# The sixth tile's down products in two matmuls instead of three, with the low half stacked beside the high half

## The chip, the cores and the metric

One core of a Trainium2 chip runs the whole program. The metric is the device time of one execution in microseconds. Before the change it is 1329.63 us, the median of 3 runs (1329.51 to 1329.85). Engines are named as in the profile: PE does matmuls (PEld its weight loads), DVE and POOL do elementwise work, ACT does activations, SP issues the DMAs.

## What is computed

A macaron block over 2048 tokens of 256 channels, in float32:

```
x = x + 0.5 * ffn(layernorm(x))
x = x + mamba2(layernorm(x))
x = x + 0.5 * ffn(layernorm(x))
ffn(x):  h = silu(x @ gate.T) * (x @ up.T);  return h @ down.T      # gate, up: 688 x 256, down: 256 x 688
```

The FFN's weights are drawn from a table of 16 values (`lut[idx]`). The change touches both FFNs and the passage from the first FFN into the Mamba part.

## The kernel before, in words

**Split products.** Every large product is made in three passes. Each operand is rounded to a high half (type fp32r) and its rest, the low half, and `split_matmul` (L35 to L40) adds hi times hi (L38), hi times lo (L39) and lo times hi (L40) in PSUM.

**The FFN.** Its 688 inner columns are six tiles of 128; the sixth (m = 5, `MT - 1`) has 48 columns and zeros behind them. Tokens come in four tiles of 512 (T). One pair of T and m is a tick, k = 6 T + m, so each FFN has 24 ticks. In tick k PE makes gate and up products of tile k (`ffn_in`, 12 matmuls of 512 columns; in a sixth tile the up columns lie in the gate tile's rows 64 to 111, so there are 6), then transposes or side work (`before_down`), and then the down products of tile k - 2 (`ffn_down(k - 2)`, 12 matmuls of 256 columns: 3 passes for each of 4 token groups of 128). ACT makes silu of the gate product and later `ffn_hidden_hi`, the high half of the product h (L668); DVE multiplies (L1129, in a sixth tile L1125 on 64 rows); POOL makes `ffn_hidden_lo` (L961). The second FFN is the class `TickFfn`, with the same split of work (L97, L103, L109, L117, L121).

**What PE waits for in the first FFN.** The up products of tick k go to the bank that silu of tick k - 1 read, so they wait for `silu_done` k (at m > 0). The transposes of the next token tile's normalised rows xn (L205; at k = 1, 3, 5) wait for DVE, which writes xn (L196) after its product of ticks 0, 2 and 4. Down products wait for the low half.

**Work woven into the first FFN.** ACT splits one Mamba weight tile, `xw_raw` to `xw_hi` (L680), after `ffn_hidden_hi` in each of ticks 0 to 3, and waits there for that tile's DMA. POOL makes `xw_lo` (L967) behind it. The buffer `xw_raw` has two places, so the loads of tiles 2 and 3 (L535) can start only when POOL is done with tiles 0 and 1. From tick 9 on Mamba's B, C and dt are made beside the FFN's ticks: projection on PE, a causal convolution on DVE (`taps_bc`, L1167 and L1171), silu on ACT.

**The queue of SP** is strictly in order. After the first loads it stores the decoded FFN weights for the second FFN (`spill`, L555: gate, up, then down_hi and down_lo), and behind these stand the loads of `xw_raw` 2 and 3.

**After tick 23** comes the passage into the Mamba loop (`fill(-8)`): turn_B and make_CB for token tile 2, the first x and gate projections, and the last layer norm: ACT's silu of CT, the rows of cum and e, B_tok, a square root (L178), then DVE's xn (L196) and PE's transposes.

## Time and profile before

| | |
|---|---|
| median of 3 runs | 1329.63 us |
| the profiled execution | 1329.74 us, its span 1328.0 us |
| PE busy | 1281.5 us, 96% |
| DVE busy | 1185.5 us, 89% |
| ACT busy | 999.6 us, 75% |
| POOL busy | 891.7 us, 67% |

Times in rows count from the span's start. The first FFN lies at 76 to 196 us, the Mamba loop between about 204 and 1219, the second FFN at 1219 to the end. A matmul's busy time is longer than the distance to the next one's start, since matmuls overlap; what one costs is read from start to start.

### The profile page before, as it was taken

How to read it: one execution, taken by the hardware profiler on the slowest of the kernel's cores; microseconds unless marked ns; L12 is line 12 of the kernel's file. 1: busy time of each engine (PE TensorE's matmuls, PEld its weight loads, DVE VectorE, ACT ScalarE, POOL GpSimd, SP SyncE). 2: the span in 40 equal slices, each digit the busy share in tenths (PEclk: the TensorE clock that was granted, in tenths of full speed). 3: DMA queues.
4: the chain of work that ended last, by engine and by line, in shares of the span. 5: the costliest groups of instructions: out<-in, count | busy, mean ns of one | idle time of the engine just before them, and what ended most of it. 6: DMA issues, size and time to landing. Idle time of an engine off the chain costs nothing.

```text
span 1328.0 us, 26759 instructions
## 1 busy us (share of the span) xinstructions
PE 1281.5 (96%) x8784; PEld 1080.8 (81%) x8784; DVE 1185.5 (89%) x2652; ACT 999.6 (75%) x2044; POOL 891.7 (67%) x920
## 2 busy tenths in 40 slices
PE   7999998899999999999999999999999999997998
PEld 7988886678888888887888888888878888876887
DVE  7965577899999999999999999999999999997542
ACT  1135567888888888888888888888888888883442
POOL 1033220279798988888797989888887979785332
PEclk9999999999999999999999999999999999998999
DMA  7031002365654643545655556445445654435000
GB/s 166 2 151 33 17 28 62 73 136 131 112 123 117 133 116 110 119 108 110 114 132 116 120 124 122 122 109 119 108 108 113 132 124 114 104 104 214 16 17 33
DMA packets 98105, 136.49 MB, mean 103 GB/s; under 512 B 23760, under 2 KB 45872, under 8 KB 97840
## 3 DMA queue, kind: packets, MB, share of 16 engines
q1 hardware_dynamic: 97968, 134.78, 42.7%
q8 instruction: 72, 1.18, 0.4%
q14 instruction: 65, 0.53, 0.1%
HBM read 124.78 MB, written 9.96 MB: 101 GB/s over the span
## 4 chain that ended last, share of the span: by engine, by line
PE 71%; DVE 17%; issue 7%; ACT 3%; POOL 1%; DMA 0%; DVEq 0%; POOLq 0%; SPq 0%; ACTq 0%
PE psum L38 15%; PE psum L40 13%; PE psum L39 13%; PE psum L1749 9%; PE psum L1726 7%; PE psum L1738 6%; PE psum L1527 4%; PE psum L1715 4%; DVE inner L1346 2%; DVE xs L1294 2%; DVE xdt L1304 2%; DVE xend L1312 2%; DVE mixed L1376 1%; DVE M L1322 1%; DVE carry L1346 1%
## 5 line engine op out<-in xcount | busy, mean ns | idle before, releaser
L848 ACT ACTIVATE M<-cum_row,cum_table 128x128 f32<-128x128 f32 x1024 | 312.1, 389 | 0.0
L1294 DVE SCALAR_TENSOR_TENSOR xs<-psum,conv_w_sb,xs 128x509 f32<-128x509 f32 (+2 forms) x384 | 282.2, 735 | 0.4
L1056 POOL TENSOR_TENSOR hid<-hid,sg 128x512 f32<-128x512 f32 x128 | 165.6, 1294 | 86.3 <-DVE hid L1363 86.3
L1007 POOL CAST hid_hi<-hid 128x512 fp32r<-128x512 f32 x128 | 194.0, 1516 | 8.2
L1042 POOL TENSOR_TENSOR squares<-squares,sq 128x512 f32<-128x512 f32 x124 | 161.1, 1299 | 53.3 <-ACT sq L825 53.3
L1322 DVE TENSOR_TENSOR M<-M,CB 128x1024 f32<-128x1024 f32 x128 | 187.7, 1467 | 0.0
L862 ACT ACTIVATE xs<-psum,conv_b_sb,conv_w_sb 128x512 f32<-128x512 f32 x128 | 99.1, 774 | 105.0 <-PE psum L40 66.9
L1010 POOL TENSOR_TENSOR hid_lo<-hid,hid_hi 128x512 fp32r<-128x512 f32 x128 | 166.2, 1299 | 10.2
L1749 PEld LDWEIGHTS psum<-M,xdt 128*64 128x64 f32 x2048 | 109.9, 137 | 45.9 <-issue 45.9
L1726 PE MATMUL psum<-xend,B_tok 128*128 128x128 f32 x960 | 132.0, 279 | 10.6 <-DVE carry L1346 9.8
L1749 PE MATMUL psum<-M,xdt 128*64 128x128 f32 x2048 | 140.8, 280 | 0.8 <-DVE psum L1354 0.7
L856 ACT ACTIVATE M<-M 128x1024 f32<-128x1024 f32 x128 | 134.5, 1051 | 0.5
L1726 PEld LDWEIGHTS psum<-xend,B_tok 128*128 128x128 f32 x960 | 117.6, 192 | 16.4 <-DVE xend L1312 8.3
L961 POOL TENSOR_TENSOR ffn_hidden_lo<-ffn_hidden,ffn_hidden_hi 128x512 fp32r<-128x512 f32 x24 | 31.2, 1301 | 132.6 <-ACT ffn_hidden_hi L668 132.6
L1346 DVE SCALAR_TENSOR_TENSOR inner<-inner,decay_table,psum 128x64 f32<-128x64 f32 x512 | 116.7, 267 | 0.0
L38 PE MATMUL psum<-xT_hi,gw_hi 128*128 128x512 f32 x256 | 111.7, 436 | 4.9 <-issue 4.9
L38 PE MATMUL psum<-xT_hi,xw_hi 128*128 128x512 f32 x256 | 113.4, 443 | 0.0
L1738 PE MATMUL psum<-CT,inner 128*128 128x128 f32 x768 | 107.2, 276 | 1.3 <-DVE inner L1346 0.8
L38 PE MATMUL psum<-hid_hi,wo_hi 128*128 128x512 f32 x256 | 100.9, 394 | 4.6 <-issue 3.9
L1738 PEld LDWEIGHTS psum<-CT,inner 128*128 128x128 f32 x768 | 97.6, 191 | 5.6 <-DVE inner L1346 2.1
L40 PE MATMUL psum<-xT_hi,xw_lo 128*128 128x512 f32 x256 | 101.1, 395 | 0.0
L40 PE MATMUL psum<-xT_hi,gw_lo 128*128 128x512 f32 x256 | 100.7, 393 | 0.0
(201 smaller groups left out, 3308.1 us busy)
## 6 DMA issues: line engine op xcount, KB each, us to landing
cum_row<-cum_scratch SPq DMA_DIRECT2D x256, 256.0 KB, 4.7
e_row<-e_scratch SPq DMA_DIRECT2D x256, 128.0 KB, 4.1
xw_raw<-L_attn_in_proj_w_dram SPq DMA_DIRECT2D x32, 128.0 KB, 4.8
wo_raw<-L_attn_out_proj_w_dram SPq DMA_DIRECT2D x32, 128.0 KB, 4.6
gw_raw<-L_attn_in_proj_w_dram SPq DMA_DIRECT2D x16, 256.0 KB, 5.0
x_res<-_attn_hidden_states_dram SPq DMA_DIRECT2D x4, 512.0 KB, 7.8
x_scratch<-x_res SPq DMA_DIRECT2D x4, 512.0 KB, 2.6
x_res<-x_scratch SPq DMA_DIRECT2D x1, 2048.0 KB, 10.5
```

Source lines behind the costliest of these rows:

```text
L38: nc.tensor.matmul(out, l_hi, r_hi, start=start, stop=False, skip_group_check=skip)
L39: nc.tensor.matmul(out, l_hi, r_lo, start=False, stop=False, skip_group_check=skip)
L40: return nc.tensor.matmul(out, l_lo, r_hi, start=False, stop=stop, skip_group_check=skip)
L848: last = nc.scalar.activation(M[:, v % 3, h, c * CH:(c + 1) * CH], cum_row[:, v % 2, h, c * CH:(c + 1) * CH], ACT.Relu, bias=scalar_of(CUM ...
L1007: nc.gpsimd.tensor_copy(hid_hi[:, v % 2, :], hid[:, v % 2, :]).then_inc(hid_hi_done, 1)
L1010: nc.gpsimd.tensor_tensor(hid_lo[:], hid[:, v % 2, :], hid_hi[:, v % 2, :].bitcast(F32), ALU.subtract).then_inc(hid_lo_done, 1)
L1056: nc.gpsimd.tensor_tensor(hid[:, v % 2, :], hid[:, v % 2, :], sg[:, v % 8, :], ALU.mult).then_inc(hid_done, 1)
L1294: nc.vector.scalar_tensor_tensor(xs[:, v % 7, shift:], psum[:, X_BANK + v % 2, 0:TT - shift], tap_of(v, step), xs[:, v % 7, shift:], ALU.m ...
L1322: nc.vector.tensor_tensor(M[:, v % 3], M[:, v % 3], cb, ALU.mult).then_inc(M_done, 1)
L1726: last = nc.tensor.matmul(psum[:, ST_BANK, c * P:(c + 1) * P], B_tok[:, t * CPT + c, :], xend[:, c].rearrange("p h q -> p (h q)"), start=T ...
L1738: last = nc.tensor.matmul(psum[:, Y_BANK, c * CH:(c + 1) * CH], before.rearrange("p h q -> p (h q)"), CT[:, tok:tok + CH], start=(c == fir ...
L1749: last = nc.tensor.matmul(psum[h * HP:(h + 1) * HP, Y_BANK, c * CH:(c + 1) * CH], xdt[:, v % 2, c, h, :], M[:, v % 3, h, c * CH:(c + 1) * CH],
```

## The change

For a sixth tile only 48 rows of h are real, so the 64 rows below them are free. ACT now writes the high half to rows 0 to 63 alone, and DVE writes the low half to rows 64 to 127 of the same tile (`ffn_tail_lo`); POOL has nothing to do there. The rows 64 to 127 of `down_hi`'s sixth tile get a copy of its rows 0 to 63, once, on DVE at k = 2; those of `down_lo` stay zero. One matmul with `down_hi` then adds hi times hi and lo times hi, a second with `down_lo` hi times lo: 8 matmuls for a sixth tile where there were 12. The store of down_hi waits for the copy (`doubled`). In `fill(-8)` the first x projection is moved ahead of turn_B and make_CB.

```
+def stacked_matmul(nc, out, both, w_hi, w_lo):
+    nc.tensor.matmul(out, both, w_hi, start=False, stop=False, skip_group_check=True)
+    return nc.tensor.matmul(out, both, w_lo, start=False, stop=True, skip_group_check=True)
...
     def pool_lo(self, pool, k):
+        if k % MT == MT - 1:
+            return
...
@@ def spill(i), on SP
                 if i == 0:
                     sp.wait_ge(tail_done, 2)
+                if i == 2:
+                    sp.wait_ge(doubled, 1)
...
@@ def ffn_hi(k), on ACT
-                nc.scalar.activation(f_hi[:, k % 3, :], f_h[:, k % 2, :], ACT.Copy).then_inc(f_hi_done, 1)
+                rows = slice(0, HP if k % MT == MT - 1 else P)
+                nc.scalar.activation(f_hi[rows, k % 3, :], f_h[rows, k % 2, :], ACT.Copy).then_inc(f_hi_done, 1)
...
@@ on DVE
+            def ffn_tail_lo(k):
+                dve.wait_ge(f_hi_done, k + 1)
+                nc.vector.tensor_tensor(f_hi[HP:P, k % 3, :], f_h[0:HP, k % 2, :], f_hi[0:HP, k % 3, :].bitcast(F32),
+                                        ALU.subtract).then_inc(tail_lo_done, 1)
...
@@ def after_mult(k)
+                if k == 2:
+                    dve.wait_ge(w_lo_done, 9)
+                    nc.vector.tensor_copy(w["down_hi"][HP:P, MT - 1, :],
+                                          w["down_hi"][0:HP, MT - 1, :].bitcast(F32)).then_inc(doubled, 1)
...
                 if k == 23:
+                    ffn_tail_lo(k)
                     taps_bc(2, 1, 7)
...
             for k in range(FFN_TICKS):
                 before_mult(k)
                 ffn_mult(k)
+                if k % MT == 0 and k > 0:
+                    ffn_tail_lo(k - 1)
...
                 ffn2.vector_mult(dve, k)
+                if k % MT == 0 and k > 0:
+                    ffn2.vector_tail_lo(dve, k - 1)
...
+            ffn2.vector_tail_lo(dve, FFN_TICKS - 1)
             ffn2.vector_add(dve, NT - 1)
...
@@ def ffn_down(k), on PE
-                pe.wait_ge(f_lo_done, k + 1)
+                if m == MT - 1:
+                    pe.wait_ge(tail_lo_done, T + 1)
+                else:
+                    pe.wait_ge(f_lo_done, ups(k))
...
+                if k == MT - 1:
+                    pe.wait_ge(doubled, 1)
                 for s in range(CPT):
+                    if m == MT - 1:
+                        last = stacked_matmul(nc, bank(4 + s // 2)[:, (s % 2) * D:(s % 2 + 1) * D],
+                                              f_hi[:, k % 3, s * P:(s + 1) * P], w["down_hi"][:, m, :],
+                                              w["down_lo"][:, m, :])
+                        continue
...
@@ def fill(s), on PE
                 if s == -8:
+                    proj_x(0)
                     turn_B(2, 6)
                     make_CB(2, 7)
-                    proj_x(0)
                     pe.wait_ge(x_done, NT)
                     proj_g(0)
```

SP's queue around the store of the down weights, of the kernel before:

```order
L555 DMA up_lo_scratch<-up_lo 128x1536
L555 DMA down_hi_scratch<-down_hi 128x1536 [waits w_lo_done,w_hi_done]
L555 DMA down_lo_scratch<-down_lo 128x1536
L535 DMA xw_raw<-L_attn_in_proj_w_dram 128x2x128 [waits loop_xw_lo_done] x2
L542 DMA gw_raw<-L_attn_in_proj_w_dram 128x2x256 [waits loop_gw_lo_done]
```

And of the changed kernel:

```order
L582 DMA up_lo_scratch<-up_lo 128x1536
L582 DMA down_hi_scratch<-down_hi 128x1536 [waits doubled,w_lo_done,w_hi_done]
L582 DMA down_lo_scratch<-down_lo 128x1536
L560 DMA xw_raw<-L_attn_in_proj_w_dram 128x2x128 [waits loop_xw_lo_done] x2
L567 DMA gw_raw<-L_attn_in_proj_w_dram 128x2x256 [waits loop_gw_lo_done]
```

The order is the same, but everything from down_hi on now stands behind the wait for `doubled`.

DVE of the changed kernel in ticks 1 to 3, where the copy that gives `doubled` stands (the second and third row of products are ticks 2 and 3):

```order
L248 TENSOR_TENSOR xT_lo<-psum,xT_hi 128x512 [waits ln1_hi_done] x2
L1161 TENSOR_TENSOR ffn_hidden<-psum,ffn_silu_gate 128x512 [waits up_done,f_lo_done,silu_done]
L220 TENSOR_SCALAR xn<-x_res,ln_mv,ln_rstd 128x256 [waits ln1_turned]
L220 TENSOR_SCALAR xn<-x_res,ln_mv,ln_rstd 128x256 x3
L1279 CAST down_hi<-down_hi 64x256 [waits w_lo_done]
L1161 TENSOR_TENSOR ffn_hidden<-psum,ffn_silu_gate 128x512 [waits up_done,f_lo_done,silu_done]
```

The cast (L1279) is the new row; it stands behind tick 2's product and the four xn rows.

DVE around tick 23's product, of the kernel before:

```order
L1171 SCALAR_TENSOR_TENSOR conv_B<-psum,conv_bc,conv_B 128x509
L1125 TENSOR_TENSOR ffn_hidden<-psum,ffn_silu_gate 64x512 [waits f_lo_done,silu_done]
L1167 SCALAR_TENSOR_TENSOR CT<-halo_bc,conv_bc,CT 128x1 [waits bc_done,bc_evac]
L1171 SCALAR_TENSOR_TENSOR CT<-psum,conv_bc,CT 128x511
L1167 SCALAR_TENSOR_TENSOR CT<-halo_bc,conv_bc,CT 128x2 [waits bc_step]
```

And of the changed kernel:

```order
L1208 SCALAR_TENSOR_TENSOR conv_B<-psum,conv_bc,conv_B 128x509
L1157 TENSOR_TENSOR ffn_hidden<-psum,ffn_silu_gate 64x512 [waits f_lo_done,silu_done]
L1165 TENSOR_TENSOR ffn_hidden_hi<-ffn_hidden,ffn_hidden_hi 64x512 [waits f_hi_done]
L1204 SCALAR_TENSOR_TENSOR CT<-halo_bc,conv_bc,CT 128x1 [waits bc_done,bc_evac]
L1208 SCALAR_TENSOR_TENSOR CT<-psum,conv_bc,CT 128x511
```

The low half (L1165), with its wait for ACT, now stands ahead of the convolution of CT.

## Rows read from the trace of the kernel before

**Rows 1.** Windows by stage: busy time of each engine, granted clock, DMA share, GB/s.

```profile
76.00:180.00 104.00, 103.82 (x600) 89.57 (x599) 66.27 (x142) 61.51 (x96) 35.56 (x31) 1.00 0.11 39
1219.00:1328.00 109.00, 103.50 (x600) 90.53 (x600) 45.49 (x110) 41.43 (x64) 31.04 (x24) 0.97 0.06 20
```

**Rows 2.** Timeline of PE, ticks 4 and 5: start us, us, what.

```profile
94.16 0.39 PE L38 MATMUL psum<-xT_hi,up_hi 128*128 128x512 f32 x1
...
95.56 0.28 PE L38 MATMUL psum<-down_hi,ffn_hidden_hi 128*128 128x256 f32 x1
...
96.86 0.28 PE L40 MATMUL psum<-down_hi,ffn_hidden_lo 128*128 128x256 f32 x1
...
99.17 0.36 PE L38 MATMUL psum<-down_hi,ffn_hidden_hi 128*128 128x256 f32 x1
```

**Rows 3.** Timeline of SP's queue, start of the first FFN.

```profile
80.22 0.32 SPq L555 DMA_DIRECT2D down_hi_scratch<-down_hi  x1
80.59 0.43 SPq L555 DMA_DIRECT2D down_lo_scratch<-down_lo  x1
83.74 4.00 SPq L535 DMA_DIRECT2D xw_raw<-L_attn_in_proj_w_dram  x2
```

**Rows 4.** DMA issues between 80 and 90 us: KB, median us to landing.

```profile
xw_raw<-L_attn_in_proj_w_dram SPq DMA_DIRECT2D x2, 128.0 KB, 2.3
```

**Rows 5.** Line L535, all 32 loads of `xw_raw`.

```profile
DMA to landing us min/median/max: 2.1/4.8/8.3
```

**Rows 6.** Timeline of ACT, ticks 2 and 3.

```profile
87.80 0.40 ACT L680 ACTIVATE xw_hi<-xw_raw 128x256 fp32r<-128x256 f32 x1
89.27 0.60 ACT L674 ACTIVATE ffn_silu_gate<-psum 128x512 f32<-128x512 f32 x1 [1.07 <-PE psum L40]
91.53 1.09 ACT L213 ACTIVATE xT_hi<-psum 128x512 fp32r<-128x512 f32 x2 [1.67 <-PE psum L205]
```

**Rows 7.** Timeline of DVE: xn of token tiles 2 and 3.

```profile
87.14 2.35 DVE L196 TENSOR_SCALAR xn<-x_res,ln_mv,ln_rstd 128x256 f32<-128x256 f32 x4
...
96.46 2.34 DVE L196 TENSOR_SCALAR xn<-x_res,ln_mv,ln_rstd 128x256 f32<-128x256 f32 x4
```

**Rows 8.** Timelines around tick 19: DVE, PE.

```profile
168.67 1.68 DVE L1208 SCALAR_TENSOR_TENSOR ez<-dt_table,a_exp 128x512 f32<-128x512 f32 x1
...
170.50 1.03 PE L1611 MATMUL psum<-ez,upper 128*128 128x512 f32 x2
```

**Rows 9.** Timeline of DVE, tick 23.

```profile
191.62 0.69 DVE L1125 TENSOR_TENSOR ffn_hidden<-psum,ffn_silu_gate 64x512 f32<-64x512 f32 x1
192.23 0.20 DVE L1167 SCALAR_TENSOR_TENSOR CT<-halo_bc,conv_bc,CT 128x1 f32<-128x1 f32 x1
...
193.24 1.11 DVE L1167 SCALAR_TENSOR_TENSOR CT<-halo_bc,conv_bc,CT 128x2 f32<-128x2 f32 x1
```

**Rows 10.** Timelines of ACT and POOL, tick 23 and after.

```profile
192.34 0.63 ACT L668 ACTIVATE ffn_hidden_hi<-ffn_hidden 128x512 fp32r<-128x512 f32 x1 [1.63 <-DVE ffn_hidden L1125]
...
196.02 0.63 ACT L712 ACTIVATE CT<-CT 128x512 f32<-128x512 f32 x1 [2.53 <-DVE CT L1171]
...
201.80 0.20 ACT L178 ACTIVATE ln_sd<-ln_ve 128x4 f32<-128x4 f32 x1
...
193.05 1.28 POOL L961 TENSOR_TENSOR ffn_hidden_lo<-ffn_hidden,ffn_hidden_hi 128x512 fp32r<-128x512 f32 x1 [4.04 <-ACT ffn_hidden_hi L668]
```

**Rows 11.** Timelines of ACT and PE, the last tile of the second FFN.

```profile
1319.73 0.63 ACT L103 ACTIVATE ffn_hidden_hi<-ffn_hidden 128x512 fp32r<-128x512 f32 x1 [0.76 <-DVE ffn_hidden L117]
...
1321.76 0.39 PE L38 MATMUL psum<-down_hi,ffn_hidden_hi 128*128 128x256 f32 x1 [0.54 <-POOL ffn_hidden_lo L109]
```

**Rows 12.** Timeline of PE, gaps before the second FFN.

```profile
1211.67 0.47 PE L38 MATMUL psum<-hid_hi,wo_hi 128*128 128x512 f32 x1 [2.89 <-issue]
...
1219.25 0.76 PE L38 MATMUL psum<-xT_hi,gate_hi 128*128 128x512 f32 x1 [2.10 <-DVE xT_lo L224]
...
1223.22 0.57 PE L38 MATMUL psum<-xT_hi,up_hi 128*128 128x512 f32 x1
```

More of the change, by code:

```diff
@@ L86, in tensor_down @@
         for s in range(CPT):
+            if m == MT - 1:
+                last = stacked_matmul(self.nc, self.bank(4 + s // 2)[:, (s % 2) * D:(s % 2 + 1) * D],
+                                      self.hi[:, k % 3, s * P:(s + 1) * P],
+                                      self.w["down_hi"][:, m, :], self.w["down_lo"][:, m, :])
+                continue
             last = split_matmul(self.nc, self.bank(4 + s // 2)[:, (s % 2) * D:(s % 2 + 1) * D],
@@ L113, in vector_mult @@
         dve.wait_ge(self.silu_done, k + 1)
-        if k >= 2:
-            dve.wait_ge(self.lo_done, k - 1)
+        if k >= 2 and (k - 2) % MT < MT - 1:
+            dve.wait_ge(self.lo_done, ups(k - 2))
+        elif k >= 2:
+            dve.wait_ge(self.tail_lo_done, (k - 1) // MT)
         if k % MT == MT - 1:
```

24 lines of the change are left out of this document (20 added, 4 removed).

## The prediction

> **What bounds the kernel now.** I read the windows by stage first: in the first FFN PE is busy 103.82 of 104.00 us at the full clock (1.00), while DVE has 66.27 and POOL 35.56 us [rows 1]. So there a matmul less is time less, until some other engine is late. In the second FFN PE has 103.50 of 109.00 us, and its gaps are at the two ends [rows 1]. The span is 1328.0 us and the execution took 1329.74 us, 1.7 us around it; the median of the runs is 1329.63, 0.1 below. What a change of the span does to one it does to the other.
>
> **What is removed.** In the rows of a down product the first of 12 matmuls starts at 95.56 and the last at 96.86 [rows 2]: 1.30 us over 11 steps, 0.118 us each. Four matmuls fewer are 0.47 us per sixth tile. There are eight such tiles.
>
> - First FFN, tiles 5 and 11: PE-bound ticks 7 and 13, so -0.47 each, -0.94. Tile 17 falls in tick 19. What follows it on PE is the cumulative sum (L1611), which started at 170.50 and needs DVE's L1208, done at 168.67 + 1.68 = 170.35 [rows 8]. So PE can gain about 0.1 there and then waits for DVE: -0.1. Tile 23 is the last, and the passage behind it is led by another chain (below): 0.
> - Second FFN, tiles 5, 11 and 17: -0.47 each, -1.41. Nothing on DVE or ACT is close to late there: DVE, busy 45.49 of 109.00 us [rows 1], gets four short operations more.
> - Second FFN, last tile: hi is done at 1319.73 + 0.63 = 1320.36, and PE starts the last down product at 1321.76, after a wait of 0.54 for POOL [rows 11]. DVE's low half has no row. The nearest is the 64x512 product at 0.69 us [rows 9]; it is SBUF only, so I bound it by 0.55 and 0.75 and take 0.69. It would end near 1321.1, which is also when PE is through with tile 22. So the start is 0.66 earlier (0.54 to 0.7), and the product 0.47 shorter: -1.1.
>
> The sum of the gains is 0.94 + 0.1 + 1.41 + 1.1 = 3.55 us.
>
> **What is added at tick 2.** The store of down_hi waits for the copy on DVE, and behind it in SP's queue stand the loads of `xw_raw` 2 and 3. Before, SP issued the store at 80.22 and the load of tile 2 at 83.74 [rows 3]. Such a load landed 2.1 us or so after its issue (median 2.3 for the two [rows 4], least 2.1 [rows 5]), so at 85.9, 5.7 us after the first store was issued, and ACT took it at 87.80 without waiting [rows 6]. Now the copy comes after xn of token tile 2, which ends at 87.14 + 2.35 = 89.49 [rows 7]. The copy is 64x256. The nearest rows are 0.20 (128x1) and 0.69 (64x512) [rows 9]; I take 0.3. SP then issues the store near 89.9 and the load near 90.7. The load's bytes follow two stores of 128x1536 floats in the same queue, so I give it the same 5.7 us from the first store: 95.6. Bounds: 2.1 us after its own issue, 92.8; or 8.3 us, the longest such load [rows 5], 99.0.
>
> Who is queued behind it on ACT: the split at 87.80 now starts near 95.6, then silu of tick 3, before at 89.27 [rows 6], now 95.9 to 96.5. PE's up product of tick 4 waits for that silu; it stood at 94.16 [rows 2]. PE waits 2.4 us. The delay then grows, as ACT has its queue to work off: the two xT_hi (1.09), hi of tick 3 (0.63 [rows 10]), the split of tile 3 (0.40), silu of tick 4 (0.60 [rows 6]), which ends near 98.75. DVE's product follows to 99.45, then xn of token tile 3, 2.34 us [rows 7], to 101.8. Before, that xn ended at 96.46 + 2.34 = 98.80, and PE had its transposes done and started the next down product at 99.17 [rows 2]. So PE is 3.0 us late from there on.
>
> POOL may add to this. Four xn rows take 2.35 us next to one POOL operation, and now two POOL operations (xw_lo of tile 3 and the low half of tick 4) fall on them. DVE rows that lie beside a POOL operation are visibly stretched: L1167 took 1.11 us where its neighbour took 0.20, and ended as POOL's 193.05 + 1.28 did [rows 9, 10]. A second catch costs up to 1.0. I take +3.5 for tick 2 (3.0 to 4.0; with the bounds of the landing 0.3 to about 7).
>
> This bears on the skill. The Trainium skill, SBUF — State Buffer, section SBUF: two separate sides, says that VectorE and GpSimd share one port pair as an exclusive lock, held for a whole instruction. By that rule the second catch is a full POOL operation and the term is 4.0; by the rows of four xn alone it is 3.0.
>
> Is anything later able to give the 3.5 back? No: PE is busy without a gap to tick 19, and the chain of DVE and ACT at tick 19 was itself started by PE's projections, so it is late by the same.
>
> **What is added at tick 23.** DVE's low half stands ahead of the convolution of CT and waits for ACT's hi, done at 192.34 + 0.63 = 192.97 [rows 10]. It runs 193.0 to 193.65, so CT starts near 193.65 where it started at 192.23 [rows 9]: +1.4. POOL's low half at 193.05 is gone, and with it the stretch of L1167 from 0.20 to 1.11: -0.9. Net +0.5 (0 to +1.4). ACT had been idle for 2.53 us for CT at 196.02, and from there goes without a pause to the square root at 201.80 [rows 10], on which the last xn and PE's transposes hang. So +0.5 passes on. The projection moved ahead of turn_B costs and brings nothing: what hides it is ACT's own work, over 5 us from CT's silu to the root [rows 10]. If that cover were gone, it would cost the six matmuls' 1.4 us (94.16 to 95.56 for six such [rows 2]).
>
> At ticks 6, 12 and 18 of each FFN DVE has the low half (0.69) as well. Its user is PE's product a tick later, over 2 us off: 0.
>
> **The sum.** -3.55 + 3.5 + 0.5 = +0.45 us: 1330.2 for the profiled execution, 1330.1 for the median.
>
> **Rivals.**
>
> *The load is hidden.* If `xw_raw` lands 2.1 us after its issue, at 92.8, silu of tick 3 ends at 93.7, before PE needs it at 94.16, and only about 0.3 is left of the 3.5. The sum is -2.75: 1326.9. For it speaks the row of 2.3 for the two loads; against it that they were issued 3.1 us after the second store, and now only 0.4 after. Chance 0.17.
>
> *The wait grows and the clock falls (slower).* If the load lands at 8.3 us, 99.0, PE waits 5.8 us instead of 2.4: +3.4. And the array may drop to its half rate. A PE gap of 2.89 us left the full rate; after gaps of which the last was 2.10, with only transposes between, the matmuls came 0.44 us apart (1219.25 to 1223.22, nine steps) and not 0.23 [rows 12], some 2 us lost over ten. Then 1333.5 to 1335.5. It decides from a landing of about 97.8 on, where the sum passes the +2.66 that can be told from no change. Chance 0.13. The Trainium skill, TensorE: Matmul & The Clock Gate, section HAM oscillation, says that waits between bursts put PE back to half rate; rows 12 show it at 1219 and not at 1211, and the forecast gap of 2.4 us is below the 2.89 that did no harm.
>
> *The two-pass product saves less than its share.* A weight load is busy 0.15 us in the mean (89.57 over 599 [rows 1]); if the loads set the pace, eight take 1.2 us and a tile saves 0.22, not 0.47. Over six tiles that is 1.5 us less gain: +1.95, 1331.6. Against it: twelve such loads pass in 1.42 us now. Chance 0.05.
>
> *The forecast*, with both new waits near their middle value: 0.65. Its own range is 1328.8 to 1331.6, from 3.0 and 0 to 4.0 and 1.4.
>
> **How the numbers follow.** 0.2% of the time is 2.66 us, about what a measurement of this kernel can tell. Faster needs under 1326.97: half of the first rival and a little of the forecast's lower tail, where tick 23 brings something and the load is early, 0.15. Slower needs over 1332.3: the second rival, 0.13, and 0.04 of the forecast's upper tail, 0.17. The rest is 0.68. The range is 1326.8 to 1332.8: it takes in the hidden load and the third rival and leaves out the long landing.
>
> **What would show it.** The store of down_hi issued near 89.9 and `xw_raw` 2 taken by ACT near 95.6; a PE gap near 94.2 of about 2.4 us with full rate behind it; the down product after the third set of transposes near 102.7 (before 99.17); eight matmuls 0.12 us apart for each sixth tile; ACT's square root 0.5 us later against tick 23's gate product than before; the last down product starting 1.4 us after hi's start and not 2.03. The prediction is wrong if the load is taken before 94, if the copy takes over a microsecond, or if the chain after tick 23 turns out to be PE's.

## The result, and the profile after

The changed kernel takes 1333.74 us, the median of 6 runs (1331.99 to 1335.61); the kernel before took 1330.21 in its 6 runs beside it (1329.51 to 1331.16). The ratio is 1.0027 with a 95% interval of 1.0016 to 1.0038: slower by 3.5 us where 0.45 was forecast. The profiled execution took 1331.99 us with a span of 1330.3 us. Its own distance from the profiled execution of before is 2.25 us, so two things have to be found: what the profile shows, and what other executions have that this one lacks. Of the six, three have a mean granted clock of 0.994 (1332.0 to 1333.2 us) and three have 0.989 or 0.990 (1334.3 to 1335.6 us).

The windows by stage of the kernel after answer to [rows 1]; the columns are the same.

```profile
76.00:180.00 104.00, 100.89 (x573) 86.67 (x572) 66.56 (x137) 58.88 (x94) 30.54 (x27) 0.98 0.11 39
1222.00:1331.00 109.00, 101.42 (x586) 88.22 (x584) 50.00 (x117) 43.23 (x67) 25.88 (x20) 0.97 0.06 20
```

In the first FFN PE is idle for 3.11 us where it was idle for 0.18, and its clock is no longer 1.00 throughout. That is tick 2. These are the timelines after of SP's queue, ACT, PE and DVE around it; they answer to [rows 3], [rows 6], [rows 2] and [rows 7].

```profile
90.35 0.32 SPq L582 DMA_DIRECT2D down_hi_scratch<-down_hi  x1
90.71 0.43 SPq L582 DMA_DIRECT2D down_lo_scratch<-down_lo  x1
91.19 2.27 SPq L560 DMA_DIRECT2D xw_raw<-L_attn_in_proj_w_dram  x2
```

```profile
96.38 0.42 ACT L708 ACTIVATE xw_hi<-xw_raw 128x256 fp32r<-128x256 f32 x1 [8.05 <-DMA xw_raw<-L_attn_in_proj_w_dram]
96.71 0.58 ACT L702 ACTIVATE ffn_silu_gate<-psum 128x512 f32<-128x512 f32 x1
```

```profile
97.34 0.51 PE L38 MATMUL psum<-xT_hi,up_hi 128*128 128x512 f32 x1 [2.56 <-ACT ffn_silu_gate L702]
...
97.95 0.63 PE L40 MATMUL psum<-xT_hi,up_lo 128*128 128x512 f32 x1
98.38 0.63 PE L38 MATMUL psum<-xT_hi,up_hi 128*128 128x512 f32 x1
...
103.19 1.03 PE L229 MATMUL psum<-ident,xn 128*128 128x128 f32 x8
103.98 0.36 PE L38 MATMUL psum<-down_hi,ffn_hidden_hi 128*128 128x256 f32 x1
```

```profile
86.98 0.69 DVE L1161 TENSOR_TENSOR ffn_hidden<-psum,ffn_silu_gate 128x512 f32<-128x512 f32 x1 [0.96 <-PE psum L40]
...
89.97 0.29 DVE L1279 CAST down_hi<-down_hi 64x256 fp32r<-64x256 f32 x1
...
100.61 2.35 DVE L220 TENSOR_SCALAR xn<-x_res,ln_mv,ln_rstd 128x256 f32<-128x256 f32 x4
...
104.02 0.69 DVE L1157 TENSOR_TENSOR ffn_hidden<-psum,ffn_silu_gate 64x512 f32<-64x512 f32 x1 [1.06 <-ACT ffn_silu_gate L702]
```

The DMA issues of the kernel after between 85 and 100 us, which answer to [rows 4]:

```profile
xw_raw<-L_attn_in_proj_w_dram SPq DMA_DIRECT2D x2, 128.0 KB, 4.9
```

The copy takes 0.29 us, the load is issued at 91.19 behind the two stores, ACT has it 6.0 us after the first store was issued, and PE waits 2.56 us for silu. Soon behind the gap matmuls of 512 columns start 0.43 us apart: half rate. From there PE works to 103.98 without a further wait: the four xn take 2.35 us, as before, and are done at 102.96, ahead of their transposes at 103.19. So from this up product to the next token tile's down product PE needs 6.64 us (97.34 to 103.98) where it needed 5.01 (94.16 to 99.17 [rows 2]). That is 1.63 us more, nearly all of it at half rate. Tick 5's product on DVE starts at 104.02 where it started at 99.21, 4.81 us later.

Not all of these 4.81 are the change's. DVE's product of tick 2, ahead of everything that the change touches, already starts at 86.98 where it started at 86.53. This offset comes from the first loads of an execution and differs each time. So I read all profiles by one ledger: how much later the same instructions of DVE start than in the profile of before. The first column is the offset at tick 2, each further one what is added from mark to mark, in us. Tick 2 is read at DVE's addition behind tick 7, with the 0.48 added back that tick 7's product saves (it stands apart in the kernel of experiment 2). The columns "half clock" are what is added from 202 to 245 us, at the passage, and from 245 to 262, at the start of the Mamba loop; it is over 0.1 only where the granted clock is 0.5 for a stretch there.

| profile | offset | tick 2 | ticks 7, 13 | tick 19 | tick 23 | half clock, passage | half clock, loop | second FFN |
|---|---|---|---|---|---|---|---|---|
| forecast | 0 | +3.5 | -0.94 | -0.1 | +0.5 | 0 | 0 | -2.51 |
| after | +0.45 | +4.36 | -0.96 | +0.15 | +0.62 | 0 | 0 | -2.46 |

The 4.36 of tick 2 are made up of PE's start, 2.73 us late (97.34 less 94.16 less the offset of 0.45), and the 1.63 us at half rate. The rest of the way, from the root to the second FFN, adds 0.1. The second FFN's ticks give back 0.40, 0.48 and 0.48 us, and its last tile 1.10. The timelines of ACT and PE at the last tile, which answer to [rows 11]:

```profile
1323.09 0.63 ACT L118 ACTIVATE ffn_hidden_hi<-ffn_hidden 64x512 fp32r<-64x512 f32 x1 [0.76 <-DVE ffn_hidden L141]
...
1324.49 0.38 PE L51 MATMUL psum<-down_hi,ffn_hidden_hi 128*128 128x256 f32 x1
```

The product starts 1.40 us after hi and not 2.03. And where PE bounds, a sixth tile is eight matmuls 0.12 us apart (timeline of PE, tick 7):

```profile
112.51 0.28 PE L51 MATMUL psum<-down_hi,ffn_hidden_hi 128*128 128x256 f32 x1
...
113.33 0.28 PE L52 MATMUL psum<-down_lo,ffn_hidden_hi 128*128 128x256 f32 x1
```

### The profile page after: what moved, and what is told of

The parts are those of the page before. It is cut to its first block, busy times and chain, and to the rows that moved or that the text cites. A ratio compares the mean times of both kernels' runs of the same rounds, so it can differ in the third digit from the quotient of the medians.

```text
span 1330.3 us, 26689 instructions
## 1 busy us (share of the span) xinstructions
PE 1281.3 (96%) x8752; PEld 1079.9 (81%) x8752; DVE 1192.5 (90%) x2661; ACT 999.4 (75%) x2044; POOL 881.7 (66%) x912
## 4 chain that ended last, share of the span: by engine, by line
PE 71%; DVE 19%; issue 5%; ACT 4%; DMA 1%; DVEq 0%; SPq 0%; POOL 0%; ACTq 0%; POOLq 0%
PE psum L38 15%; PE psum L40 13%; PE psum L39 13%; PE psum L1806 8%; PE psum L1783 7%; PE psum L1795 6%; PE psum L1574 4%; PE psum L1772 3%; DVE xs L1336 2%; DVE inner L1388 2%; DVE xdt L1346 2%; DVE xend L1354 2%; DVE mixed L1418 1%; DVE M L1364 1%; DVE carry L1388 1%
## 5 line engine op out<-in xcount | busy, mean ns | idle before, releaser
L991 POOL TENSOR_TENSOR ffn_hidden_lo<-ffn_hidden,ffn_hidden_hi 128x512 fp32r<-128x512 f32 x20 | 26.2, 1311 | 127.4 <-ACT ffn_hidden_hi L696 127.4
```

## The experiments

My first theory, A: the array's idleness of 2.56 us brought its clock down, and the half rate behind it (twelve matmuls, some 1.5 us) is what the forecast of tick 2 lacked. Each kernel ran beside the kernel before on the same chip; "before" is the median of the runs of before in that comparison.

### 1. The wait alone

The kernel before, three passes everywhere, with the copy (of zeros onto themselves) and the wait.

```diff
                 if i == 0:
                     sp.wait_ge(tail_done, 2)
+                if i == 2:
+                    sp.wait_ge(doubled, 1)
...
+                if k == 2:
+                    dve.wait_ge(w_lo_done, 9)
+                    nc.vector.tensor_copy(w["down_hi"][HP:P, MT - 1, :],
+                                          w["down_hi"][HP:P, MT - 1, :].bitcast(F32)).then_inc(doubled, 1)
```

> The kernel before, all down products in three passes, with nothing added but DVE's copy at tick 2 (it copies the padding rows of down_hi, which are zero, onto themselves, so nothing of the computation changes), the wait of down_hi's store for it and PE's wait for it at tick 5. Theory A (the tick 2 stall costs a wait of about 2.5 us on PE, and the granted clock then falls to half for a stretch, which adds about 1.5 to 2 us): slower by 4 to 6 us, 1334.2 to 1336.2, with a granted clock of 0.5 right behind PE's gap near 94. Rival B (the stall alone costs the 3.0 to 3.5 forecast, and the rest of the changed kernel's median comes from elsewhere, the two-pass products among it): slower by 3.0 to 3.5 us, and the clock stays 1.0 behind the gap.

Measured: 1335.35 us (1334.75 to 1336.01, 5 runs) against 1330.15, ratio 1.0037 (1.0024 to 1.0049). Tick 2 adds 4.35 us, as in the changed kernel, and nothing else in the first FFN moves. The timeline of PE:

```profile
96.50 0.79 PE L38 MATMUL psum<-xT_hi,up_hi 128*128 128x512 f32 x1 [2.56 <-ACT ffn_silu_gate L677]
97.09 0.63 PE L39 MATMUL psum<-xT_lo,up_hi 128*128 128x512 f32 x1
```

The whole stall is the wait in SP's queue, and the half rate stands behind PE's gap, as theory A said. The 5.2 us at the median lie in its 4 to 6, but partly by luck: a further 1.54 us comes at 245 to 262, in a part of the program that this kernel shares with before to the letter. This was not expected, and experiments 4, 10 and 11 are about it.

### 2. The loads ahead of the store

```diff
-            for i in range(len(ORDER)):
+            for i in range(len(ORDER) - 1):
                 spill(i)
             for p in range(2, GP):
                 load_x_weights(p)
+            spill(len(ORDER) - 1)
```

> The changed kernel with one move in SP's program: the two loads of xw_raw 2 and 3 stand ahead of the stores of down_hi and down_lo. Nothing else changes. Theory A: tick 2 costs nothing, PE has no gap near 94 and its clock stays 1.0 there, and the gains (0.96 at ticks 7 and 13, 1.36 in the second FFN, 1.1 at the last tile) less 0.6 at tick 23 remain: 2.5 to 2.9 us under the kernel before, ratio 0.9978 to 0.9981, 4.4 to 6 under the changed kernel. Rival B: the spread of the changed kernel's executions has another cause, and it stays: only 3 to 3.5 us are gained on the changed kernel, ratio 0.9995 to 1.0005 with executions 3 us apart.

Measured: 1329.23 us (1326.41 to 1330.80, 11 runs) against 1330.15, ratio 0.9990 (0.9982 to 0.9999), 3.4 us under the changed kernel beside it (experiment 4). The timeline of SP's queue:

```profile
83.80 4.00 SPq L560 DMA_DIRECT2D xw_raw<-L_attn_in_proj_w_dram  x2
90.39 0.34 SPq L582 DMA_DIRECT2D down_hi_scratch<-down_hi  x1
```

Tick 2 adds 0.00 us and PE has no gap there, as theory A (and any theory of the queue) said. But the median is 0.9 us under before, 1.6 us short of even the lower end of its 2.5 to 2.9. The two shortest executions, 1326.41 and 1326.66 us, have a mean clock of 0.995; the other nine have 0.991 to 0.993. Rival B had that part right: another cause of spread stays, and 3.4 us are gained on the changed kernel where it said 3 to 3.5.

### 3. The copy ahead of xn

```diff
+                if k == 2:
+                    dve.wait_ge(w_lo_done, 9)
+                    nc.vector.tensor_copy(w["down_hi"][HP:P, MT - 1, :],
+                                          w["down_hi"][0:HP, MT - 1, :].bitcast(F32)).then_inc(doubled, 1)
                 if k in (0, 2, 4):
                     ln1.vector_normalise(dve, k // 2 + 1)
...
-                if k == 2:
-                    dve.wait_ge(w_lo_done, 9)
-                    nc.vector.tensor_copy(w["down_hi"][HP:P, MT - 1, :],
-                                          w["down_hi"][0:HP, MT - 1, :].bitcast(F32)).then_inc(doubled, 1)
```

> The changed kernel with DVE's copy ahead of xn of token tile 2 instead of behind it, so that the stores and loads behind it on SP are issued 2.35 us earlier. By the 5.95 us from the first store's issue to ACT's split, xw_raw 2 lands near 94.0 instead of 96.3, and PE's gap shrinks from 2.56 to about 0.2. Theory A (the gap brings the clock down): with so short a gap the clock stays 1.0, and the kernel comes within 0.5 us of the one with the loads ahead, 2.0 to 2.9 us under the kernel before. Rival C (the clock falls in any case because the engine was less busy ahead of it, the gap's length does not matter): the granted clock of 0.5 is there all the same, and the kernel stays 0.5 to 1 us around the kernel before.

Measured: 1332.09 us (1330.37 to 1332.94, 11 runs) against 1330.15, ratio 1.0012 (1.0003 to 1.0020). The landing and the gap came as expected, and the clock stayed up:

```profile
94.43 0.50 PE L38 MATMUL psum<-xT_hi,up_hi 128*128 128x512 f32 x1 [0.30 <-ACT ffn_silu_gate L702]
```

Yet tick 2 adds 2.25 us, where theory A had at most 0.5. PE's start is only 0.46 us late (94.43 plus 0.19 less 94.16), and it is held behind it, by xn (timelines of DVE and PE):

```profile
97.30 3.68 DVE L220 TENSOR_SCALAR xn<-x_res,ln_mv,ln_rstd 128x256 f32<-128x256 f32 x4
```

```profile
101.04 0.44 PE L229 MATMUL psum<-ident,xn 128*128 128x128 f32 x2 [0.83 <-DVE xn L220]
```

Three POOL operations lie beside the four xn, which take 3.68 us and not 2.35, and PE waits 0.41 and 0.83 us for them. So a late load costs PE 1.8 us behind the gap at the full clock too. The load is issued 2.3 us earlier than with the wait alone, and the delay is 2.1 us less. That is a first mark against theory A; rival C, a fall of the clock here in any case, is out as well.

### 4. The changed kernel again

> The changed kernel once more, unchanged, to see whether its wide spread (1332.0 to 1335.6 over six executions, where the kernel before has 1.65 us) repeats, and to have a second profile. Theory A with the clock: the stretch at half rate behind the gap differs from one execution to the next; executions come again over 3 us or so, median 3 to 4 us over the kernel before, and if the profile is of a long one, it shows a longer or further stretch at 0.5 near 98. Rival B: the spread sits elsewhere (the loads at the start, or the start of the second FFN), and a long execution's profile shows it there, with the stretch near 98 as in the first profile, 3.4 us.

No edit. Measured: 1332.67 us (1331.06 to 1333.82, 11 runs) against 1330.15, ratio 1.0017 (1.0008 to 1.0026). The stretch at half clock behind tick 4 is the same one, and tick 2 adds 4.13. The windows from 200 to 260 us, first profile and this one (the number before the last two is the granted clock):

```profile
200.00:260.00 60.00, 47.56 (x265) 36.30 (x263) 50.83 (x117) 45.38 (x82) 5.68 (x11) 1.00 0.31 80
```

```profile
200.00:260.00 60.00, 49.49 (x259) 38.35 (x259) 49.33 (x115) 44.41 (x81) 5.71 (x11) 0.94 0.36 79
```

Here the clock falls at 208.07, behind the transposes of the last layer norm, and 1.58 us are added between 202 and 215; the first profile had none of it. Not every such stretch costs: a second one at 242.2 adds 0.03 us. What tells the two profiles apart lies there and not at tick 4.

### 5. The gap filled

The changed kernel with the wait left as long as it is, and PE kept busy through it (FILL is 20).

```diff
+                    if (what, k) == ("up", 4):
+                        pe.wait_ge(f_lo_done, ups(2))
+                        for n in range(FILL):
+                            nc.tensor.matmul(bank(4)[:, 0:D], f_hi[HP:P, 2, 0:P], w["down_lo"][HP:P, MT - 1, :],
+                                             start=False, stop=False, skip_group_check=True)
                     if what == "up" and k >= 1:
                         pe.wait_ge(silu_done if m > 0 else h_done, k)
```

> The changed kernel with 20 extra matmuls on PE between gate(4) and the wait for silu(3), of 0.12 us each: they add the low half of tile 2 times the zero padding rows of down_lo to the accumulator, so nothing of the output changes, and they fill the gap of 2.56 us. The wait for ACT stays as long as it was. Theory A (the array's idleness brings the clock down): the clock stays 1.0 behind tick 4, up(4) and down(2) take the 0.24 and 0.12 us a matmul of the kernel before, and down(3) starts about 3.0 to 3.4 us later than before and not 4.4: 1.0 to 1.4 us under the changed kernel. Rival G (the clock falls for another reason than idleness, or the xn chain sets the delay anyway): the rows of half rate are there, or are gone and down(3) starts 4.4 us late all the same; no gain on the changed kernel.

Measured: 1333.21 us (1331.62 to 1336.04, 8 runs) against 1330.32, ratio 1.0023 (1.0012 to 1.0033). The timeline of PE and, below, those of DVE and POOL:

```profile
95.22 2.65 PE L1599 MATMUL psum<-down_lo,ffn_hidden_hi 64*128 64x256 f32 x20
97.83 0.50 PE L38 MATMUL psum<-xT_hi,up_hi 128*128 128x512 f32 x1
...
98.40 0.39 PE L40 MATMUL psum<-xT_hi,up_lo 128*128 128x512 f32 x1
98.63 0.39 PE L38 MATMUL psum<-xT_hi,up_hi 128*128 128x512 f32 x1
...
103.16 0.44 PE L230 MATMUL psum<-ident,xn 128*128 128x128 f32 x2 [0.40 <-DVE xn L221]
104.43 0.44 PE L230 MATMUL psum<-ident,xn 128*128 128x128 f32 x2 [0.83 <-DVE xn L221]
```

```profile
100.70 3.67 DVE L221 TENSOR_SCALAR xn<-x_res,ln_mv,ln_rstd 128x256 f32<-128x256 f32 x4
```

```profile
100.60 0.74 POOL L998 TENSOR_TENSOR xw_lo<-xw_raw,xw_hi 128x256 fp32r<-128x256 f32 x1
101.53 1.42 POOL L992 TENSOR_TENSOR ffn_hidden_lo<-ffn_hidden,ffn_hidden_hi 128x512 fp32r<-128x512 f32 x1 [0.19 <-ACT ffn_hidden_hi L697]
102.91 1.31 POOL L1004 TENSOR_TENSOR gw_lo<-gw_raw,gw_hi 128x512 fp32r<-128x512 f32 x1
```

The clock stays up, with matmuls 0.23 us apart, so the idleness does bring it down. But tick 2 adds 4.51 us all the same, 0.15 more than with half clock: rival G's second half. Theory A is right on what PE does in the changed kernel, 1.63 us at half rate with no wait for xn, and falls as an account of what the stall costs without it, for behind the half rate lies a second limit. At the full clock PE is early enough that DVE starts xn sooner against POOL's work (3.8 us after ACT has the load, and not 4.2), and then three POOL operations fall on the four xn, which take 3.67 us and not 2.35; PE waits for them. From the up product to the next down product PE needs 6.79 us here and 6.64 in the changed kernel. Half clock and POOL are alternatives that happen to cost about the same.

### 6. One of POOL's operations moved away

The kernel of experiment 5 with the split of gw behind the wo split of the next tick.

```diff
-                elif k - 1 in G_TICKS:
-                    split_g_lo(G_TICKS.index(k - 1))
+                elif k - 1 == G_TICKS[1]:
+                    split_g_lo(1)
                 elif k - 1 in WO_TICKS:
                     split_wo_lo(WO_TICKS.index(k - 1))
+                if k - 1 == 5:
+                    split_g_lo(0)
```

> The kernel with the filled gap, and POOL's split of gw (1.3 us) behind the wo split of the next tick and not behind the low half of tile 4, where it fell on the last xn of token tile 3. Theory H (at the full clock the tick 2 delay is 4.25 us because three POOL operations fall on the four xn, which take 3.67 us and not 2.35): the fourth xn takes 0.4 to 0.7 and not 1.35, the four end about 0.9 us earlier, the tick 2 delay is 3.2 to 3.5 us, and the median is 0.7 to 1.0 us under the filled gap. Rival I (xn is slow for another reason, or the transposes are held by PE's own work): the delay stays at 4.2.

Measured: 1332.37 us (1330.54 to 1334.37, 11 runs) against 1330.88, ratio 1.0014 (1.0005 to 1.0023). The timeline of DVE:

```profile
99.73 2.72 DVE L221 TENSOR_SCALAR xn<-x_res,ln_mv,ln_rstd 128x256 f32<-128x256 f32 x4
```

The four xn take 0.95 us less, and tick 2 adds 3.55 and not 4.51 (at tick 5's product, where the expectation was read, 3.29 and not 4.25). Theory H is shown. With the clock up and one POOL operation gone, the delay is 0.6 to 0.8 us less than in the profiles with half rate, 4.13 to 4.36. A POOL operation that meets an xn holds it to its own end: in experiment 5, POOL is done at 102.95 and 104.22, and the third and fourth xn 0.15 us after each. The Trainium skill, SBUF — State Buffer, section SBUF: two separate sides, says that the two engines share a port pair under an exclusive lock, held for a whole instruction; the trace agrees at these two ends.

### 7. The projection back behind make_CB

In this experiment and in 9 and 11 the loads stand ahead of the store, as in experiment 2.

```diff
                 if s == -8:
-                    proj_x(0)
                     turn_B(2, 6)
                     make_CB(2, 7)
+                    proj_x(0)
```

> The kernel with the loads ahead of down_hi's store, and proj_x(0) back behind turn_B and make_CB, where it stood before the change. The last layer norm's transposes wait for DVE either way. Theory D (the six matmuls moved forward leave PE idle for 2.95 us instead of 1.55 ahead of those transposes, and the granted clock then falls to half for 3.4 us in most executions, as in three of the four profiles with that order): the gap is 1.6 or less, no row of 0.5 near 204, and the median is 0.6 to 0.9 us under the kernel with the loads ahead, 1.5 to 1.9 under the kernel before. Rival E (the fall there is a matter of the moment at which the execution reaches the passage, not of the order): a stretch of 0.5 near 204 with the short gap too, and the median within 0.3 us of the kernel with the loads ahead.

> The kernel with the loads ahead and proj_x(0) back, once more, to stand on the same chip as the next: again 2.2 to 3.0 us under the kernel before, ratio 0.9977 to 0.9983.

Measured: 1327.59 us (1326.32 to 1328.57, 10 runs) against 1330.32, ratio 0.9980 (0.9971 to 0.9989), and in the second comparison 1328.20 (1327.75 to 1329.34, 11 runs) against 1330.88, again 0.9980 (0.9971 to 0.9989). PE's wait ahead of the last layer norm's transposes, in the kernel before, in the changed kernel and here (timelines of PE):

```profile
203.60 1.32 PE L205 MATMUL psum<-ident,xn 128*128 128x128 f32 x8 [1.55 <-DVE xn L196]
```

```profile
208.21 0.56 PE L229 MATMUL psum<-ident,xn 128*128 128x128 f32 x3 [2.95 <-DVE xn L220]
```

```profile
202.61 0.56 PE L229 MATMUL psum<-ident,xn 128*128 128x128 f32 x3 [1.55 <-DVE xn L220]
```

The median is 2.7 us under before, where the kernel of experiment 2 was 0.9 under: 1.8 us for a move that the forecast gave nothing. Theory D is right on the sign and the gap; it gave the move 0.6 to 0.9 us. The 1.8 comes from two comparisons on different chips, each with an interval of about 1.2 us to either side, so its size is rough. Of the six profiles with the gap of 2.95, three have half clock behind it, adding 1.2 to 1.6 us; of the eleven with 2.0 us or less there, none has it behind the gap. The counts are small, but in the same direction. In experiment 2 it looked so (timeline of PE; at full rate the eight transposes are busy 1.32 us):

```profile
203.46 1.94 PE L229 MATMUL psum<-ident,xn 128*128 128x128 f32 x8 [2.95 <-DVE xn L220]
205.05 0.78 PE L38 MATMUL psum<-xT_hi,gw_hi 128*128 128x512 f32 x1
```

### 8. The projection moved alone

The kernel before, with `proj_x(0)` ahead of turn_B and make_CB, the reverse of the diff above.

> The kernel before with one edit: proj_x(0) ahead of turn_B and make_CB, as in the changed kernel. Theory D (the PE gap ahead of the last layer norm's transposes grows from 1.55 us by the six matmuls' 1.39, and the granted clock falls behind it in part of the executions, which costs 1.2 to 1.6 us when it does): gap 2.9 to 3.0, median 0.5 to 1.2 us over the kernel before, and single executions up to 1.5 us longer than its longest. The forecast's step (the move costs nothing, as ACT's chain hides it): within 0.3 us of the kernel before.

Measured: 1329.89 us (1329.05 to 1332.30, 11 runs) against 1330.88, ratio 0.9996 (0.9987 to 1.0005). The timeline of PE:

```profile
204.24 1.31 PE L205 MATMUL psum<-ident,xn 128*128 128x128 f32 x8 [2.02 <-DVE xn L196]
```

The gap is 2.02 us and not 2.9, and no half clock follows. From tick 23's down product to the transposes the kernel before has waits of 0.58, 0.19 and 1.55 us, 2.3 in all, so there is little more to gather into one; the changed kernel has 0.53 and 2.95. Theory D misses for the move alone, and the forecast's step holds there: by the profiles the loss needs the move and the two-pass product together.

### 9. The low half of tile 23 one step later

The kernel of experiment 7 with DVE's low half behind the first tap of CT's convolution.

```diff
                 if k == 23:
-                    ffn_tail_lo(k)
                     taps_bc(2, 1, 7)
...
+                    if (T, bc, step) == (2, 1, 0):
+                        ffn_tail_lo(FFN_TICKS - 1)
```

> As the kernel with the loads ahead and proj_x(0) back, and DVE's low half of tile 23 one step later: behind the first tap of CT's convolution and not ahead of it. The wait for ACT's hi (0.65 us after the product) then lies behind 0.95 us of convolution. Theory A with the forecast's tick 23 term: CT is 0.6 to 0.7 us earlier than with the low half ahead, all gains of the two-pass products remain, 2.2 to 3.4 us under the kernel before, ratio 0.9974 to 0.9983. Rival F (CT is not what the passage waits for): within 0.2 us of the kernel with proj_x(0) back.

> The kernel with tile 23's low half behind CT's first tap, once more. Its first profile has the 0.8 us of tick 23 that was expected, and loses 1.6 us to stretches at half clock near 225 and 249 that the other's profile lacks. If these come by the moment of the execution, the order of the two kernels' medians can turn, and this one is 0.3 to 0.8 us under the one before it; if the place of the low half brings them on (PE waits 0.91 us for CT and not 1.92, with the cumulative sums nearer to it), it is again 0 to 0.6 us over it, with clocks of 0.992 in half of its executions.

Measured: 1328.21 us (1326.09 to 1329.89, 11 runs) against 1330.32, ratio 0.9981 (0.9972 to 0.9990); again 1328.39 (1326.65 to 1329.40, 11 runs) against 1330.88, 0.9982 (0.9973 to 0.9991). The timeline of DVE:

```profile
192.92 0.69 DVE L1166 TENSOR_TENSOR ffn_hidden_hi<-ffn_hidden,ffn_hidden_hi 64x512 fp32r<-64x512 f32 x1
193.63 0.22 DVE L1205 SCALAR_TENSOR_TENSOR CT<-halo_bc,conv_bc,CT 128x2 f32<-128x2 f32 x1
```

Tick 23 now adds -0.17 us in both profiles, where it added 0.62: the 0.8 us are real. But both profiles lose 1.6 us to half clock near 250, and 14 of 22 executions have clocks of 0.991 to 0.993 (5 of 21 in experiment 7). At the median this version is not to be told from that of experiment 7, though it has the shortest execution of all, 1326.09 us. The mean clock marks such a stretch only roughly: the first of these profiles has it at a mean of 0.994.

### 10. The kernel before, again, and later by filler

> The kernel before once more, for a second profile. Its 27 executions on this chip spread over 2.9 us. If the stretches of 0.5 near 229 to 257, seen in profiles of the kernel with the wait alone and of two others, hang on the moment and not on the change, some profile of the kernel before can show one too (costing 0.7 to 0.9 us each); near 97 and near 204 it should show none, as PE has gaps of at most 0.2 and 1.55 us there.

Measured: 1330.23 us (1329.46 to 1331.47, 11 runs), ratio 1.0000 (0.9992 to 1.0009), clock 1.00 from 200 to 260 us, as in the first profile. So the kernel before does not lose there in either profile. To find whether the change brings that on, filler was put into tick 8 of the kernel before, and nothing else: SHIFT matmuls, 12 in one kernel and 29 in another.

```diff
+                if k == 8:
+                    for n in range(SHIFT):
+                        nc.tensor.matmul(bank(4)[:, 0:D], f_hi[HP:P, 2, 0:P], w["down_lo"][HP:P, MT - 1, :],
+                                         start=False, stop=False, skip_group_check=True)
                 for s in range(CPT):
```

> The kernel before, with 12 matmuls more ahead of the down product of tick 8, of 0.118 us each (they add the low rows of the hidden tile times zero padding, so the output stays): everything from tick 8 on comes 1.4 us later, and nothing of the change is in it. Theory J (a gap brings the clock down or not by the moment at which the execution comes to it; the kernel before comes at a good moment): half of the executions or more have stretches at 0.5 between 200 and 260, as the kernel with the wait alone had at 229 and 253, clocks of 0.991 to 0.993, and the median is 2.0 to 3.2 us over the kernel before. Rival K (the gaps of the changed passage bring it on): no such stretch, clock 0.995, and the median is 1.3 to 1.6 us over.

> The same with 29 matmuls: 3.4 us later from tick 8 on, as late as the changed kernel was in its first profile (3.9 at tick 23), which had no stretch at half clock in the passage. Theory J: as there, few or none in the passage, clock 0.994 to 0.995, 3.3 to 3.9 us over the kernel before, so that 17 matmuls more cost less than their 2.0 us against the kernel with 12. Rival K: 3.4 us over, 2.0 over the kernel with 12.

Measured with 12: 1333.44 us (1331.46 to 1334.65, 9 runs) against 1329.82, ratio 1.0025 (1.0015 to 1.0035). With 29: 1334.55 us (1333.01 to 1335.92, 5 runs), ratio 1.0036 (1.0024 to 1.0049). PE's wait in front of the place, in the kernel before and with 12 (timelines of PE):

```profile
248.41 1.13 PE L1726 MATMUL psum<-xend,B_tok 128*128 128x128 f32 x8 [2.00 <-DVE carry L1346]
```

```profile
251.81 1.13 PE L1731 MATMUL psum<-xend,B_tok 128*128 128x128 f32 x8 [1.99 <-DVE carry L1347]
```

The windows around 250 us with 12, and with 29:

```profile
249.00:257.00 8.00, 6.01 (x38) 4.81 (x40) 7.79 (x18) 3.99 (x5) 3.00 (x3) 0.79 0.19 55
```

```profile
249.00:257.00 8.00, 5.57 (x45) 4.25 (x43) 7.97 (x19) 4.12 (x5) 3.15 (x3) 1.00 0.28 64
```

With 12 the filler itself adds 1.80 us and half clock near 253 another 1.54, and the clocks of the nine executions are 0.991 to 0.994. With 29 the filler adds 3.83 and the profile has no half clock there, with clocks of 0.993 to 0.995. So 17 matmuls more add 2.03 us in the ledger and 1.1 at the median. Both medians are above theory J's ranges, 2.0 to 3.2 and 3.3 to 3.9. A filler cost more than its 0.118 us a matmul, and with 29 some 0.9 us at the median have no place in the profile. Theory J is shown in its main point: a kernel without anything of the change, with the same wait of PE, loses at the loop's start with nothing but filler put some 125 us ahead of it. That it does so by some amounts and not by others rests on one profile of each. And the lateness alone does not decide it. At 245 us experiment 6 is 3.30 us later than before and has no half clock at the loop's start, the kernel with 12 fillers is 3.40 later and has it; experiment 8 is 0.62 later without, experiment 7's second profile 0.44 later with it. What decides is left open.

### 11. The first FFN's sixth tiles back in three passes

The kernel of experiment 7 with tile 5, 11, 17 and 23 as before, except that the three matmuls take 64 rows of the tile (the rows below hold the copy now).

```diff
+                        last = split_matmul(nc, bank(4 + s // 2)[:, (s % 2) * D:(s % 2 + 1) * D],
+                                            f_hi[0:HP, k % 3, s * P:(s + 1) * P], f_lo[0:HP, k % 3, s * P:(s + 1) * P],
+                                            w["down_hi"][0:HP, m, :], w["down_lo"][0:HP, m, :],
+                                            start=False, stop=True, skip=True)
```

> The kernel with the loads ahead and proj_x(0) back, but the sixth tiles of the first FFN in three passes with POOL's low half, as before the change; the second FFN keeps its two passes. By the ledger of the profiles the first FFN's two-pass products bring 0.96 at ticks 7 and 13 and cost 0.15 at tick 19 and 0.62 at tick 23: this kernel is 0.2 us (0 to 0.5) over the one with them, 2.2 to 2.7 under the kernel before. Rival (the forecast's terms: 0.94 and 0.1 gained, 0.5 lost): 0.5 over. If tick 23 is what brings the stretches at half clock on, this one has fewer and is 0.3 us or more under.

Measured: 1330.38 us (1329.11 to 1330.88, 11 runs) against 1329.82, ratio 1.0004 (0.9995 to 1.0012). This misses, by 3 us against experiment 7, and does not answer its question, for two reasons. Products over 64 rows between products over 128 cost PE more than their share (0.38 us for one group, below; tile 5 comes out 0.20 and tile 11 0.38 us longer than before), so the first FFN came out 1.15 us longer than before and 1.33 longer than in experiment 7, where 0.2 was expected. And the profile has half clock near 251, which adds 1.56. What the first FFN's two passes are worth has to be read from the ledger.

## Why the prediction was wrong, point by point

The ledger of the experiments, columns as above. What the columns leave out, the rest of the way, is -0.2 to +0.9 us; the 0.9 of experiment 4 come mostly inside the loop and were not traced.

| profile | offset | tick 2 | ticks 7, 13 | tick 19 | tick 23 | half clock, passage | half clock, loop | second FFN |
|---|---|---|---|---|---|---|---|---|
| 1 wait alone | -0.39 | +4.35 | 0 | 0 | 0 | 0 | +1.54 | +0.1 |
| 2 loads first | +0.07 | 0 | -0.96 | +0.14 | +0.62 | +1.20 | +1.55 | -2.46 |
| 3 copy before xn | -0.19 | +2.25 | -0.97 | +0.16 | +0.61 | +1.38 | 0 | -2.46 |
| 4 changed kernel | -0.92 | +4.13 | -0.96 | +0.15 | +0.62 | +1.58 | 0 | -2.52 |
| 5 gap filled | +0.94 | +4.51 | -0.96 | +0.15 | +0.61 | 0 | 0 | -2.47 |
| 6 gw later | -0.02 | +3.55 | -0.97 | +0.15 | +0.62 | 0 | 0 | -2.53 |
| 7 projection back | -0.80 | 0 | -0.96 | +0.15 | +0.62 | 0 | 0 | -2.51 |
| 7 again | +0.64 | 0 | -0.96 | +0.15 | +0.62 | 0 | +1.63 | -2.52 |
| 9 low half later | +0.54 | 0 | -0.97 | +0.15 | -0.17 | 0 | +1.59 | -2.47 |
| 9 again | +0.59 | 0 | -0.96 | +0.15 | -0.17 | 0 | +1.60 | -2.53 |

**Right.** The mechanism of tick 2 up to PE's gap: the copy at 0.3 (0.29), the load issued near 90.7 (91.19, less the offset of 0.45), its landing 5.7 us after the first store (6.0), PE's gap of 2.4 us (2.56). The wait alone (experiment 1) brings the whole delay of tick 2. The 5.7 was partly luck: before, 3.5 us of it passed until SP issued the load (80.22 to 83.74) and 2.1 until it landed; now it is issued 0.84 us after the first store and takes 4.9 us to land. The two-pass product saves its share: -0.96 at ticks 7 and 13 (-0.94 forecast), -1.36 at the second FFN's three tiles (-1.41), -1.10 at the last (-1.1), started 1.40 us after hi (1.4). Tick 23 costs 0.62 (0.5), inside its bounds. The hidden load, the rival that would have been faster, did not happen, and the third rival, of weight loads setting the pace, did not either.

**Mis-sized and failed: the term of tick 2**, "I take +3.5 for tick 2 (3.0 to 4.0", measured 4.36, 4.13 and 4.35 in three profiles. The step that failed is what follows PE's gap. The forecast kept the full clock there, as "the forecast gap of 2.4 us is below the 2.89 that did no harm", which rested on one row, and let DVE's xn set the end. In the changed kernel the clock fell, and PE's own matmuls set the end: 2.73 us of late start and 1.63 at half rate, with xn (2.35 us, so the second catch by POOL cost nothing) ready in time. Some 0.3 of the late start is the landing. The wrong moral would be that without the fall the 3.0 to 4.0 would have held. With the gap filled the clock stays up and tick 2 adds 4.51, as "A second catch costs up to 1.0" is too little there: three POOL operations fall on the four xn, which take 3.67 us. So both limits were priced too low, and they come out alike by luck. By its own terms, 3.0 and 0 to 4.0 and 1.4, the forecast's narrow range is 1329.1 to 1331.5 and not 1328.8 to 1331.6, which changes nothing.

**Failed: "Its user is PE's product a tick later, over 2 us off: 0"**, for the low halves at ticks 6, 12 and 18. At tick 18 the user is not what counts. Behind the 0.69 us on DVE stands the chain to the cumulative sums that PE waits for at tick 19: +0.15 where -0.1 was forecast. The timeline of DVE after, which answers to [rows 8]:

```profile
170.62 0.68 DVE L1165 TENSOR_TENSOR ffn_hidden_hi<-ffn_hidden,ffn_hidden_hi 64x512 fp32r<-64x512 f32 x1
...
172.66 1.67 DVE L1245 SCALAR_TENSOR_TENSOR ez<-dt_table,a_exp 128x512 f32<-128x512 f32 x1
```

**Failed: "The projection moved ahead of turn_B costs and brings nothing"**. That ACT's chain hides its 1.4 us is right (experiment 8). But taken out of PE's last wait, they make the gap 2.95 and not 1.55 together with the shorter product, and behind 2.95 half the profiles show half clock, on the chain that sets the time. Putting it back gave 1.8 us at the median, as far as two comparisons can tell.

**Left out: the other executions.** The ledger of the profile sums to +1.8 us: 4.36 - 0.96 + 0.15 + 0.62 - 2.46 + 0.1. The first comparison measured +3.5 and the second +2.5. What is between is, by all that the profiles show, half clock at the passage and at the loop's start, 1.2 to 1.6 us each time, in part of the executions; the long ones of the first comparison, with mean clocks of 0.989 and 0.990, have no profile. The kernel before loses none there in its two profiles, and none of its executions in the comparisons has a mean clock under 0.993; the fillers of experiment 10 show that filler alone, far ahead, can bring it on. The forecast, made from one profile to another, could not have this in its sum; its range could, and did not. Why the two comparisons of the changed kernel differ by 1 us is not settled. The rival with a falling clock named the right event and the right time, 1333.5 to 1335.5, but by a late load that did not come; that its time fits is luck.

## What to carry to other kernels

- A wait put into an in-order DMA queue delays every load behind the transfer that needed it. Move the loads ahead first: here this one move of two lines, with the projection where it was, turns a change that costs 3.5 us into one that brings 2.7.
- Price a stall to the end of the backlog, not to the end of the gap, and on each path: PE at half rate lost 1.63 us behind the gap, and with the clock kept up four xn beside POOL's work took 3.67 us where they had taken 2.35. To lift the half rate alone won nothing.
- Before work is taken out of an engine's wait, look at how long that makes the wait, not only at whether something hides it; and take the spread over executions, with their clocks, as part of the result when a term is smaller than 2 us.

## What the runs showed that I had not expected

- The kernel before has no half clock at the loop's start in its profiles, and it is easily brought to it. 1.80 us of filler in a PE-bound tick cost 3.6 us at the median, and 3.83 us of filler 4.7.
- PE pays for a change of the rows it works on. The timeline of PE with 12 filler matmuls over 64 rows, whose neighbours go over 128:

```profile
125.33 0.39 PE L40 MATMUL psum<-xT_hi,w_bc_lo 128*128 128x512 f32 x1
125.65 1.68 PE L1566 MATMUL psum<-down_lo,ffn_hidden_hi 64*128 64x256 f32 x12
127.27 0.39 PE L38 MATMUL psum<-down_hi,ffn_hidden_hi 128*128 128x256 f32 x1
127.49 0.28 PE L39 MATMUL psum<-down_lo,ffn_hidden_hi 128*128 128x256 f32 x1
```

  On the way in two starts are 0.32 us apart and the first two fillers 0.22, on the way out it is 0.21 and behind it 0.22, where 0.23, 0.12, 0.12 and 0.12 are usual. These four make 0.38 us more, and with twelve times 0.118 that is the 1.80 that the ledger has for them.
- The offset that an execution brings along from its first loads was between -0.9 and +1.6 us in the profiles. A comparison of two profiles needs a mark ahead of the change.
